# Row maxima of 1024 scores read in one piece, and two rings of PSUM banks, in the attention stage of a twelve-stage transformer kernel

## The reference, cut to what matters

```python
qkv = x @ w_qkv                                   # x: (4, 1024, 128), H = 16 heads of 8
q = q * cos + rotate_half(q) * sin                # the same for k
dots = jnp.einsum('bhid,bhjd->bhij', q, k) * scale
attn = jax.nn.softmax(dots, axis=-1)              # rows of 1024
out = jnp.einsum('bhij,bhjd->bhid', attn, v)
return out.transpose(0, 2, 1, 3).reshape(b, n, H * hd) @ w_out + b_out
```

## Time and profile before

| | |
|---|---|
| median of 3 runs | 2775.77 us (2768.81 to 2781.05) |
| span of the profiled execution (all of it that the page gives) | 2799.2 us |
| PE, DVE, ACT, POOL busy in it | 79%, 72%, 51%, 33% |
| attention stage in it | first score product at about 977 us, last copy at about 1737 us |
| DVE reduction, line 1970 | x1024, 637.0 us busy |
| ACT exponential, line 1870 | x1024, 541.9 us busy |

### The profile page before, as it was taken

One profiled execution on the slowest core, in us unless ns is written; L12 is line 12 of the kernel. 1 busy time (PEld: TensorE's weight loads), 2 busy tenths in 40 slices (PEclk: granted clock), 3 DMA queues, 4 the chain that ended last, 5 costly groups with the idle time before them and its releaser, 6 DMA issues. The chain is left out here.

```text
span 2799.2 us, 44395 instructions
## 1 busy us (share of the span) xinstructions
PE 2204.0 (79%) x13492; PEld 1373.2 (49%) x13492; DVE 2006.5 (72%) x5066; ACT 1429.6 (51%) x3079; POOL 927.7 (33%) x982
## 2 busy tenths in 40 slices
PE   3399788858967698888888887859957697788886
PEld 3389577747955212222222223548936597533334
DVE  4466688865655699999999992656658565678884
ACT  2266222115644458888888885326633365533332
POOL 4644345443432410010110100554426544323330
PEclk9999899968989879999999998969969699889998
DMA  5122100002220310000000000012221122200001
GB/s 160 45 62 64 44 23 24 15 20 54 64 76 23 116 75 21 19 18 21 19 18 19 18 10 32 29 39 62 64 66 37 47 63 78 64 0 0 0 1 31
DMA packets 110486, 115.18 MB, mean 41 GB/s; under 512 B 21776, under 2 KB 93552, under 8 KB 109488
## 3 DMA queue, kind: packets, MB, share of 16 engines
q1 hardware_dynamic: 91936, 76.13, 9.4%
q0 software_dynamic: 17280, 35.69, 3.8%
q10 hardware_dynamic: 1040, 0.53, 0.1%
HBM read 67.30 MB, written 44.57 MB: 40 GB/s over the span
## 5 line engine op out<-in xcount | busy, mean ns | idle before, releaser
L1970 DVE TENSOR_REDUCE attn_mx<-bank 128x1 f32<-128x512 f32 x1024 | 637.0, 683 | 42.8 <-PE bank L1747 41.7
L1870 ACT ACTIVATE attn_pT<-bank 128x512 f32<-128x512 f32 x1024 | 541.9, 595 | 124.5 <-PE bank L1762 122.9
L1747 PE MATMUL bank<-attn_K,attn_Q 48*128 48x512 bf16 x1024 | 334.4, 398 | 109.8 <-DVE attn_mx L1970 92.7
L1762 PE MATMUL bank<-attn_Q,attn_K 51*128 51x512 bf16 x1024 | 321.0, 387 | 3.5 <-ACT attn_pT L1870 3.5
L1747 PEld LDWEIGHTS bank<-attn_K,attn_Q 48*128 48x128 bf16 x1024 | 76.6, 94 | 429.5 <-DVE attn_mx L1970 357.5
L1775 PE MATMUL bank<-attn_pT,attn_vb 128*32 128x512 f32 x2048 | 276.4, 612 | 0.1
L1930 POOL TENSOR_TENSOR attn_m_rem<-attn_m_rem,attn_m_parts 8x128 f32<-8x128 f32 x128 | 53.4, 417 | 649.0 <-ACT attn_m_parts L1883 649.0
L2740 POOL TENSOR_TENSOR mix_rS<-mix_rT,mix_S 128x512 f32<-128x512 f32 x64 | 82.2, 1285 | 172.4 <-DVE mix_S L2795 75.6
L1016 PE MATMUL bank<-mix_prod_qk,ident 128*128 128x256 f32 x512 | 123.8, 397 | 0.0
L1016 PEld LDWEIGHTS bank<-mix_prod_qk,ident 128*128 128x128 f32 x512 | 103.5, 203 | 31.3 <-issue 17.4
L829 POOL DMA_INDIRECT y_rows<-ffn0b_ys,ffn0b_to_row x71 | 68.0, 958 | 96.7 <-DVE ffn0b_ys L860 96.1
(11 more groups left out here) (616 smaller groups left out, 5683.7 us busy)
## 6 DMA issues: line engine op xcount, KB each, us to landing
w<-in_L_w SPq DMA_DIRECT2D x4, 2048.0 KB
ffn0a_x_ring<-xs_rows SPq DMA_DIRECT2D x71, 65.0 KB
ffn0b_x_ring<-xs_rows SPq DMA_DIRECT2D x71, 65.0 KB
ffn2a_x_ring<-xs_rows SPq DMA_DIRECT2D x71, 65.0 KB, 1.8
ffn2b_x_ring<-xs_rows SPq DMA_DIRECT2D x71, 65.0 KB, 1.8
mix_in_y_back<-y_rows SPq DMA_DIRECT2D x8, 512.0 KB
ffn1a_in_y_back<-y_rows SPq DMA_DIRECT2D x8, 512.0 KB
ffn2a_y_back<-y_rows SPq DMA_DIRECT2D x8, 512.0 KB
```

The source lines that it names most:

```text
L1747: nc.tensor.matmul(a_bank[n % 3][:], slot(net.Q, h, 0, KROWS)[:, qt * P:(qt + 1) * P], slot(net.K, h, 0, KROWS)[:, hf * CH:(hf + 1) * CH], ...
L1762: nc.tensor.matmul(s_bank[n % 3][:], slot(net.K, h, 0, KROWS + MROWS)[:, kt * P:(kt + 1) * P], slot(net.Q, h, 0, KROWS + MROWS)[:, hf * CH ...
L1870: nc.scalar.activation(pT[:, p_at(b, h, kt), hf * CH:(hf + 1) * CH], s_bank[(n * HPB + hf) % 3][:], ACT.Exp, scale=HD ** -0.5).then_inc(ex ...
L1970: nc.vector.tensor_reduce(mx[:, h % 2, qt, hf:hf + 1], a_bank[n % 3][:], AX.X, ALU.max).then_inc(a_used, 1)
```

## The change

All of it lies in `attention_stage`, besides the eight banks being one PSUM tensor now, so that an instruction can read two neighbours.

- Maxima: the two `big` products of a tile go into a pair of neighbouring banks, and DVE takes the negated maximum of 128 x 1024 at once, 8 reductions per unit in place of 17. `mx` is gone.
- Two rings. Ring *a* (emptied by DVE) has two pairs, `bank[0:2]` and `bank[2:4]`; ring *s* (emptied by ACT) has three single banks, `bank[4]`, `[5]`, `[7]`. `a_place` and `s_place` number everything that passes through a ring: `a` takes score rows, gathered sums and projected outputs, `s` takes scores, the turned maxima, the turned outputs and the turned norm. A place is free when the one two (ring a) or three (ring s) before it is emptied. `bank[7]` is thus no bank apart any more, and `end_taken` is gone.
- The split of the maxima into three bf16 parts is done on POOL before the turn (`split_max`: five operations on 128 x 8, each waiting for the one before), PE turns all three at once with a bf16 matmul (24 x 128) in tile 2 in place of 1, and ACT copies them out once (`keep_max`).
- End of a sequence: all six steps stand behind tile 6 of their head on PE, ACT and DVE; the bias is added on POOL in place of DVE.

```diff
-        NMRING = 2
+        NMRING = 3
...
+        TURN_AT, GATHER_AT, END_AT = 2, 4, 6
...
-        a_bank, s_bank = net.bank[0:3], net.bank[3:6]
-        pv_bank, small_bank = net.bank[6], net.bank[7]
...
+        def a_bank(n):
+            return net.banks[:, 2 * (n % 2):2 * (n % 2) + 2, :]
+        def s_bank(n):
+            return net.bank[(4, 5, 7)[n % 3]]
...
+        for u in range(UNITS):
+            b, h = divmod(u, H)
+            for kt in range(TPB):
+                if u + LEAD < UNITS:
+                    a_place["row", *divmod(u + LEAD, H), kt] = len(a_place)
+                for hf in range(HPB):
+                    s_place["score", b, h, kt, hf] = len(s_place)
+                if kt == TURN_AT and u + 1 < UNITS:
+                    s_place["max", *divmod(u + 1, H)] = len(s_place)
+                if kt == GATHER_AT and u > 0 and closes((u - 1) % H):
+                    a_place["sums", *divmod(u - 1, H)] = len(a_place)
+                if kt == END_AT and b > 0:
+                    if h in (0, 1):
+                        s_place["o", b - 1, h] = len(s_place)
+                    if h in (2, 3):
+                        a_place["y", b - 1, h - 2] = len(a_place)
+                    if h in (5, 7):
+                        s_place["xn", b - 1, h // 7] = len(s_place)
...
         def _(pe):
+            def take_a(n):
+                need(pe, a_used, n - 1)
+                return a_bank(n)
+            def take_s(n):
+                need(pe, s_used, n - 2)
+                return s_bank(n)
             def big(b, h, qt, hf):
-                n = ((b * H + h) * TPB + qt) * HPB + hf
-                need(pe, a_used, n - 2)
...
+                n = a_place["row", b, h, qt]
+                out = take_a(n) if hf == 0 else a_bank(n)
...
+                if hf == HPB - 1:
+                    ins.then_inc(a_ready, 1)
             def turn(b, h):
                 v = b * H + h
-                pe.wait_ge(nm_ready, v + 1)
-                need(pe, m_ready, v)
-                need(pe, o_ready, closed(v - 3))
-                nc.tensor.transpose(nm_rows, nm[:, v % NMRING, :], net.ident[:]).then_inc(nm_turned, 1)
+                out = take_s(s_place["max", b, h])
+                pe.wait_ge(nm_split, v + 1)
+                nc.tensor.matmul(out[0:MCOLS, 0:P], mcols[:, v % NMRING].rearrange("p n q -> p (n q)"), ident16[:],
+                                 start=True, stop=True).then_inc(s_ready, 1)
             def small(b, h, kt, hf):
...
-                need(pe, exp_ready, n - 3 + 1)
+                out = take_s(s_place["score", b, h, kt, hf])
...
-                        if kt == 1:
-                            if last:
-                                pv(*last, PAIRS - 1)
-                            if not is_first(b) and h > 0:
-                                end_taken(b - 1, h - 1)
-                            if turned:
-                                turn(*turned)
+                        if kt == 1 and last:
+                            pv(*last, PAIRS - 1)
+                        if kt == TURN_AT and turned:
+                            turn(*turned)
                         if kt >= 3 and kt % 2 == 1:
                             pv(b, h, (kt - 3) // 2)
-                        if kt == 4 and last and closes(last[1]):
+                        if kt == GATHER_AT and last and closes(last[1]):
                             gather(*last)
-                    if not is_first(b):
-                        end_of_sequence(b - 1, h)
+                        if kt == END_AT and not is_first(b):
+                            end_of_sequence(b - 1, h)
...
         def _(act):
+            def keep_max(b, h):
+                n = s_place["max", b, h]
+                need(act, m_rows[h % 2], (b * (H // 2) + h // 2) * 16 * MROWS)
+                act.wait_ge(s_ready, n + 1)
+                nc.scalar.activation(mparts[:, h % 2, :], s_bank(n)[0:MCOLS, 0:P], ACT.Copy).then_inc(s_used, 1)
...
         def _(pool):
+            def split_max(b, h):
+                v = b * H + h
+                steps = Chain(pool, split_step, 4 * v)
+                parts, left = mcols[:, v % NMRING], nm[:, v % NMRING, :]
+                if v >= NMRING:
+                    pool.wait_ge(s_ready, s_place["max", *divmod(v - NMRING, H)] + 1)
+                pool.wait_ge(a_used, a_place["row", b, h, TPB - 1] + 1)
+                for n in range(MROWS - 1):
+                    steps.then(nc.gpsimd.tensor_copy(parts[:, n, :], left))
+                    steps.wait()
+                    steps.then(nc.gpsimd.tensor_tensor(rem[:, n, :], left, parts[:, n, :], ALU.subtract))
+                    steps.wait()
+                    left = rem[:, n, :]
+                nc.gpsimd.tensor_copy(parts[:, MROWS - 1, :], left).then_inc(nm_split, 1)
...
             def end_of_sequence(b, h):
+                if h in (2, 3):
+                    add_bias(b, h - 2)
                 if h in (3, 5):
                     norm.rstd_pow(pool, chunk(b, h // 5))
...
         def _(dve):
             def largest(b, h, qt):
-                v = b * H + h
-                for hf in range(HPB):
-                    n = (v * TPB + qt) * HPB + hf
-                    dve.wait_ge(a_ready, n + 1)
-                    nc.vector.tensor_reduce(mx[:, h % 2, qt, hf:hf + 1], a_bank[n % 3][:], AX.X, ALU.max).then_inc(a_used, 1)
-                if qt == TPB - 1:
-                    need(dve, nm_turned, v - 1)
-                    dve.wait_ge(a_used, (v + 1) * TPB * HPB)
-                    nc.vector.tensor_reduce(nm[:, v % NMRING, :], mx[:, h % 2], AX.X, ALU.max, negate=True).then_inc(nm_ready, 1)
+                v, n = b * H + h, a_place["row", b, h, qt]
+                if qt == 0:
+                    need(dve, nm_split, v - NMRING + 1)
+                dve.wait_ge(a_ready, n + 1)
+                nc.vector.tensor_reduce(nm[:, v % NMRING, qt:qt + 1], a_bank(n).rearrange("p a t -> p (a t)"), AX.X, ALU.max,
+                                        negate=True).then_inc(a_used, 1)
...
-                if qt == 0 and h in (3, 4):
-                    c = chunk(b, h - 3)
+                if qt == END_AT and h in (2, 3):
+                    c, n = chunk(b, h - 2), a_place["y", b, h - 2]
...
-                if qt == 1 and h in (3, 4):
-                    c = chunk(b, h - 3)
-                    x3 = net.x[:, bass.ds(c * CH, CH)].rearrange("p (t d) -> p t d", d=D)
-                    b_out = bcast(net.L1_bout[:].rearrange("p (a d) -> p a d", a=1), [P, TPC, D])
-                    dve.wait_ge(y_added, c + 1)
-                    nc.vector.tensor_tensor(x3, x3, b_out, ALU.add).then_inc(norm.x_whole, 1)
```

More of the change, by code:

```diff
@@ L129, in open_net @@
     n.euler = sb("euler", [P, TPC])
-    n.bank = [st.enter_context(nc.psum_tensor(f"bank{i}", [P, 512], F32)) for i in range(8)]
+    n.banks = st.enter_context(nc.psum_tensor("bank", [P, 8, 512], F32))
+    n.bank = [n.banks[:, i, :] for i in range(8)]
     n.L0_rw, n.L2_rw = sb("L0_rw", [P, E]), sb("L2_rw", [P, E])
@@ L1726, in body @@
                     if fetched:
-                        need(sp, s_ready, (b * H + h) * TPB * HPB)
+                        last = before(b, h)
+                        if last:
+                            sp.wait_ge(s_ready, s_place["score", *last, TPB - 1, HPB - 1] + 1)
                         load_head(net, sp, q_parts, k_parts, *fetched)
@@ L1808, in end_of_sequence, with turn_norm @@
+                ins.then_inc(a_ready, 1)
+            def turn_norm(b, hf):
+                out = take_s(s_place["xn", b, hf])
+                pe.wait_ge(norm.xn_ready, chunk(b, hf) + 1)
+                rows = norm.turned_rows(chunk(b, hf))
+                for i in range(TPC):
+                    ins = nc.tensor.transpose(out[:, i * P:(i + 1) * P], rows[:, i, :], net.ident[:])
+                ins.then_inc(s_ready, 1)
             def end_of_sequence(b, h):
-                if h in (0, 1, 2, 3, 5, 7):
-                    pe.wait_ge(o_ready, closed(min((b + 1) * H + h, B * H) - 1))
@@ L1816, in end_of_sequence @@
                 if h in (5, 7):
[L1817 to L1826, removed]
+                    turn_norm(b, h // 7)
             def body(b):
@@ new lines, in keep_norm, with spread @@
+            def keep_norm(b, hf):
+                n = s_place["xn", b, hf]
+                act.wait_ge(s_ready, n + 1)
+                nc.scalar.activation(norm.view(dest, chunk(b, hf)), s_bank(n).rearrange("p (t d) -> p t d", d=D),
+                                     ACT.Copy).then_inc(s_used, 1)
+            def spread(b, hf, i):
+                c = chunk(b, hf)
+                if i == 0:
+                    act.wait_ge(norm.shift_ready, c + 1)
+                    if c > 0:
+                        act.wait_ge(s_ready, s_place["xn", *divmod(c - 1, HPB)] + 1)
+                rows, x = norm.turned_rows(c), norm.view(net.x, c)
```

(7 more changed lines are left out.)

169 lines of the change are left out of this document (88 added, 81 removed).

## The result

The changed kernel takes 2771.27 us (median of 15 runs, 2764.94 to 2776.09) against 2775.77 us for the kernel before (15 runs, 2768.81 to 2788.26). The ratio is 0.9973, with a 95% interval of 0.9961 to 0.9986: faster by 4 to 11 us. The forecast was 2778 us, 2 us on the other side.

What follows compares the result with a forecast made beforehand. The prediction took a PE, ACT, PE loop through three banks, 2.49 us a pair, as the bound. Its terms, 7+4-7-2.5+0.85, made about +2.5 us on 2775.8, so 2778 us, range 2740 to 2803.

Steps and rivals of the forecast that it cites:

- the length of a pair: Plain pair of tiles in the attention loop: a PE, ACT, PE loop through three banks, 2.49 us, kept after the change.
- reduction of 1024, start to start: DVE's wide maxima in ring a: 1.13 us apart if only elements count, at most 1.36; value 0 in plain pairs.
- first pair loses, pair with the turn gains: Each unit: tiles 0 and 1 lose 0.38 us, tiles 2 and 3 gain 0.49; +7 us over 62 units.
- a gather adds to its unit: Gather in ring a: its pair 3.46 us for 3.09, next 2.49 for 2.76, `evacuate` about 0.09; +4 us for 23 gathers.
- end of a sequence, heads 0 to 8: Steps of a finished sequence in the loop: cost 6.3 us in place of 8.7, three times, -7 us.
- rows ahead of the loop: 24 score rows before the loop, where DVE sets the pace: 27.1 us, up to 28.5, for 30.4; -2.5 us.
- after the last unit: Stretch after the loop: projection 1.6 us earlier, but bias on POOL adds 0.6 and delays the first power; +0.85 us.
- split on POOL: Five operations on 128 x 8 before the turn, 1 to 6.6 us, within a unit of 10.35 us; value 0.
- The place of the maxima in ring s: Tile 2: the fourth `small` waits for the second exponential, not the first; that pair lasts 2.98 us.
- A: Rival for the loop: DVE's pace is the bound, 9.85 to 9.05 us a unit; about 2720 us, chance 0.13.
- B: Rival for tile 2: the maxima's place costs only the turn, about 0.2 us; about 2754 us, chance 0.15.
- C: Rival for ring a: the wide reduction costs as much as two, 1.36 us a row; 2800 us, chance 0.12.

## Why the prediction was wrong, step by step

**The step that failed** is the length of a pair: "Together 2.45 us, or 2.49 us in the loop's body", kept for the changed kernel. The structure was right. The term 0.52 us from the first `small` to its exponential was mis-sized: I read it as the price of running beside `big`, but it is the price of the signal on that `big`, which the change drops. The last three units have neither `big` nor its signal, so they could not tell the two apart. Measured: 0.49 us and a pair of 2.46; with the signal put back 0.51 and 2.48, worth 5.1 us over the loop. What remains to 2.49 is under 0.01 us a pair, the length by which DVE's own loop outran the other (2.48 with DVE at half width). A unit without a gather went from 10.35 to 10.32 us in place of 10.46, and this alone turned the sign: 62 units at +0.11 were 7 us, at -0.03 they are -2 us. With the rest as measured, and the units as forecast, the stage would have come out some 2 us longer than before.

**The other terms.**

| term | predicted | measured |
|---|---|---|
| reduction of 1024, start to start | 1.13 us | 1.14 us |
| first pair loses, pair with the turn gains | -0.38, +0.49 | -0.41, +0.46 (2.87 to 2.46, 2.49 to 2.95) |
| a gather adds to its unit | +0.19 over 0.87 | +0.26 (11.45-10.32 = 1.13) |
| end of a sequence, heads 0 to 8 | 6.3 for 8.7 us | 5.9 for 8.7 us (102.17 less 6 x 10.32 and 3 x 11.45) |
| rows ahead of the loop | -2.5 us | -1.5 us (first `big` to first `small`) |
| after the last unit | +0.85 us | -0.9 us |
| split on POOL | nothing | nothing (five operations of 0.19 to 0.20 us each) |

The place of the maxima in ring s came as forecast, with the second exponential releasing the fourth `small`; the earlier trace rows against the pair shown above, and the run with the turn in tile 1 shows its price. The rows ahead took what the forecast had as its upper case, 28.5 us for 24 rows, a saving of 1.9. Wide reductions there run 1.19 us apart on average, not 1.14; that two products at the half clock come late for every second one fits the rows and was not tried:

```profile
978.17 29.70 DVE L2048 TENSOR_REDUCE attn_nm<-bank 128x1 f32<-128x1024 f32 x25 [10.94 <-PE bank L1795]
```

(29.70 less 1.22, over 24.) The other 0.4 us of the saving is lost at the start, where the first reduction waits for two products: it starts 1.04 us after the first `big`, where it started after 0.63. The stretch after the last unit had both steps as put (bias and power on POOL together cost 2.3 us, by the run with the bias on DVE), but I left out the clock. Windows around it, before and after (columns as in the earlier trace rows, the clock ahead of the last two):

```profile
1715.00:1738.00 23.00, 12.14 (x58) 7.87 (x58) 6.27 (x26) 7.69 (x17) 2.01 (x2) 0.60 0.00 0
```

```profile
1709.00:1731.00 22.00, 9.10 (x58) 5.84 (x59) 4.90 (x24) 7.81 (x17) 4.51 (x4) 0.75 0.00 0
```

In the kernel before the turns and projections fall into the 1.2 GHz level and 8 projection matmuls take 2.07 us; after, 16 of them take 2.02 us at the full clock:

```profile
1715.51 2.02 PE L1854 MATMUL bank<-L_wout,attn_oT 128*128 128x128 f32 x16 [0.40 <-ACT attn_oT L1934]
```

Three other runs weigh this term: with the code after the last unit as in the changed kernel but an early fall of the clock, the stretch takes 21.60 us (turn in tile 1), 21.88 (ends in tile 7) and 22.12 (two reductions per row), against 21.64 before. So at a like clock the change gives nothing or costs up to 0.5 us there, where I had put 0.85, and the 0.9 us gained are the clock's. Why the clock held out longer was not tried.

The same goes for the ends of sequences, which I had also reckoned without the clock. In the kernel before it fell in head 4 of each of the three, for 3.4, 6.8 and 3.4 us, in the changed one in none, and in none of the two variants that keep its order on PE (the signal added, the bias on DVE). The second of these units took 14.50 us and the others 13.56 and 13.51, so 3.4 us at the 1.2 GHz level cost about 1 us there, and the three falls together about 4 us (an estimate, taken in proportion). That is half of what the ends of sequences gained (2.3, 3.5 and 2.3 us over heads 0 to 8), and most of what the loop did. The same six microseconds of both traces:

```profile
1234.00:1240.00 6.00, 5.79 (x34) 1.04 (x32) 5.04 (x10) 5.12 (x13) 0.00 (x0) 0.72 0.01 2
```

```profile
1234.00:1240.00 6.00, 5.64 (x37) 1.17 (x36) 5.54 (x5) 5.60 (x14) 2.15 (x7) 1.00 0.11 32
```

**The rivals.** A, DVE's pace as the bound, is out by two runs: DVE at half width leaves the pair at 2.48 us, and two narrow reductions per row leave it at 2.46. B, the maxima's place for the price of the turn alone, is out as well: 2.95 us for the pair. Its price becomes true when the turn moves one tile ahead. C is out by the 1.14 us.

**Where the relief of DVE went.** DVE's busy time fell by 31 us for the maxima (637.0 to 605.7 us) and by the 64 small reductions. Almost all of it became idle time before scores that PE could not yet deliver, in plain pairs because PE stood behind an exponential. The stage gained 0.41 us at the start of each unit: 0.18 of it is DVE's late first row, as the run at half width shows, and the rest fits the f32 turn, which left that pair. This was spent again on the maxima's place in the ring, 0.46 us in each of 62 units. What stayed came from the dropped signal, from the rows ahead, and from the ends of sequences, there in good part through the clock.

## What to carry to other kernels

Before a busy engine is made faster, look for a stretch of the same loop in which it has nothing to do (here the last three units); if the period is the same there, its waits are shared with another loop, and the relief is worth nothing in that period. It can still be worth much elsewhere (at half width DVE gave back 36 us ahead of the loop, at gathers and at ends of sequences, part of it through the clock), and such a stretch may lack more than that engine's work, here the other score products and their signals. Close that loop by hand, through each bank and each in-order queue, and then ask of every instruction that is put into the ring whose release it now makes late: one short matmul cost 0.49 us in one place and 0.03 us one tile earlier. In a loop that sets the period, try dropping signals that nobody needs: here one of them cost 0.1 us in each unit. And where a change gains a few microseconds, compare the granted clock stretch by stretch before calling the gain the work of the change.

## What the runs showed of the hardware that I had not expected

Of two matmuls that start 3 ns apart, a signal on the first delays that of the second: the semaphore event came 0.430 us after the product's start in place of 0.405, and the waiting ACT instruction started after 0.51 us in place of 0.49, even though nobody waited for the first signal. Two narrow reductions per row did not change that figure, so it is not DVE's reading. A reduction over two PSUM banks costs no more than its elements, 1.14 us from start to start for 1024 against 0.60 for 512. The Trainium skill, Vector Engine (DVE) Microarchitecture Reference, section 5.2, gives about 1.04 ns per column and 75 ns per instruction; worked out from that, an estimate of 1.14 us for 1024 and 0.61 for 512, and the trace agrees.
